# Setup of a two-block transformer kernel: small loads on a second queue, weights and modulation moved into the first turn

## The reference, cut to what matters

```python
# first block
tp = gelu(cond) @ Wt + bt
scale, shift = split(tp, 2)
h = layer_norm(x, ln1_g, ln1_b) * (1 + scale) + shift
q, k, v = split_heads(h @ Wqkv)
scores = q @ k.T / sqrt(16) - torus_dist * torus_scale[head]
x = x + merge(softmax(scores) @ v) @ Wout
x = x + gelu(layer_norm(x, ln2_g, ln2_b) @ W1 + b1) @ W2 + b2
# second block
ada = silu(cond @ ada1_w + ada1_b) @ ada2_w + ada2_b
shift1, scale1, gate1, shift2, scale2, gate2 = split(ada, 6)
a = attention(x, mask) @ proj_w + proj_b
x = x + gate1 * (layernorm(a) * (1 + scale1) + shift1)
m = gelu(x @ fc1_w + fc1_b) @ fc2_w + fc2_b
x = x + gate2 * (layernorm(m) * (1 + scale2) + shift2)
```

## Time and profile before

| | |
|---|---|
| runs before | 1455.85 us median of 3 (1454.34 to 1459.1) |
| the profiled execution | 1457.03 us, span of the trace 1455.2 us |
| granted TensorE clock, mean | 0.978 |
| first score matmul of turn 0 | 43.21 us |
| first score matmul of turn 1 | 127.69 us |
| TensorE busy over the span | 1309.6 us (90%) |
| HBM read and written | 72.64 MB, 58.75 MB |

### The profile page before, as it was taken

One profiled execution on the slowest core, in us unless ns is written; L12 is line 12 of the kernel. 1 busy time (PEld: TensorE's weight loads), 2 busy tenths in 40 slices (PEclk: granted clock), 3 DMA queues, 4 the chain that ended last, 5 costly groups with the idle time before them and its releaser, 6 DMA issues. The chain is left out here.

```text
span 1455.2 us, 24552 instructions
## 1 busy us (share of the span) xinstructions
PE 1309.6 (90%) x8789; PEld 1004.0 (69%) x8789; DVE 803.2 (55%) x2240; ACT 770.5 (53%) x1262; POOL 757.1 (52%) x939
## 2 busy tenths in 40 slices
PE   4898999999999999999999997989888898988777
PEld 3676777777777777777777775666666666665556
DVE  3766645645646656656645643464655556454452
ACT  3565665665665765665655752544544353453522
POOL 3788876776776776776776761020413222140323
PEclk9999999999999999999999998999999999999988
DMA  8432222223213213213213215353424242433100
GB/s 258 130 127 57 71 84 72 73 75 83 74 64 89 75 58 88 78 55 88 79 54 110 92 41 164 113 152 108 151 67 145 61 155 93 123 116 86 45 2 29
DMA packets 98259, 133.98 MB, mean 92 GB/s; under 512 B 16802, under 2 KB 51498, under 8 KB 98130
## 3 DMA queue, kind: packets, MB, share of 16 engines
q1 hardware_dynamic: 96850, 131.80, 30.3%
q10 hardware_dynamic: 1280, 0.53, 0.2%
HBM read 72.64 MB, written 58.75 MB: 90 GB/s over the span
## 5 line engine op out<-in xcount | busy, mean ns | idle before, releaser
L617 POOL TENSOR_SCALAR shifted<-shifted,row_max 128x512 f32<-128x512 f32 x512 | 360.6, 719 | 220.1 <-DVE row_max L1380 218.2
L1380 DVE CUSTOM_DVE_ANT_0 shifted<-score,bias 128x512 f32<-128x512 f32 x512 | 332.7, 687 | 255.4 <-PE score L855 165.6
L1091 ACT ACTIVATE probs<-turned 128x512 f32<-128x512 f32 x512 | 278.2, 596 | 211.4 <-PE turned L867 209.8
L867 PE MATMUL turned<-ident,shifted 128*128 128x128 f32 x2048 | 270.0, 275 | 6.8 <-POOL shifted L617 6.0
L867 PEld LDWEIGHTS turned<-ident,shifted 128*128 128x128 f32 x2048 | 233.6, 141 | 55.6 <-issue 26.6
L783 PE MATMUL dense<-w_down,hidden 128*128 128x256 f32 x1024 | 253.3, 383 | 0.8 <-ACT hidden L1072 0.8
L610 POOL TENSOR_SCALAR bias<-dist,scale 128x1024 f32<-128x1024 f32 x192 | 220.0, 1146 | 13.6 <-DMA down_bias<-in_L_cond_b 13.6
L855 PE MATMUL score<-k_rows,q_rows 97*128 97x512 f32 x512 | 205.2, 456 | 22.1 <-DVE row_max L1380 10.1
L783 PEld LDWEIGHTS dense<-w_down,hidden 128*128 128x128 f32 x1024 | 185.6, 191 | 32.6 <-issue 9.6
L763 PE MATMUL dense<-feat_m,w_up 128*128 128x512 f32 x768 | 188.4, 400 | 3.5 <-ACT hidden L1072 1.8
L763 PEld LDWEIGHTS dense<-feat_m,w_up 128*128 128x128 f32 x768 | 144.3, 192 | 37.1 <-ACT hidden L1072 5.3
(11 more groups left out here) (138 smaller groups left out, 1497.3 us busy)
## 6 DMA issues: line engine op xcount, KB each, us to landing
qk_rows<-qk_high SPq DMA_DIRECT2D x128, 256.0 KB
q_rows<-qk_rows SPq DMA_DIRECT2D x64, 384.0 KB
qk_rows<-qk_low SPq DMA_DIRECT2D x64, 256.0 KB
k_rows<-qk_rows SPq DMA_DIRECT2D x68, 192.0 KB
x_in_t<-in_x SPq DMA_DIRECT2D x8, 512.0 KB, 3.8
x_res<-in_x SPq DMA_DIRECT2D x8, 512.0 KB, 5.5
x_mid<-x_norm SPq DMA_DIRECT2D x8, 512.0 KB, 3.3
x_in_t<-x_mid SPq DMA_DIRECT2D x8, 512.0 KB, 3.9
```

The lines of the kernel that those rows point to most:

```text
L617: ins = pool.tensor_scalar(shifted[:, u % 3, i, :], shifted[:, u % 3, i, :], -1.0, row_max[:, t % 6:t % 6 + 1], ALU.mult, ALU.add)
L867: mm = pe.transpose(turned_bank[z % 2][:, HALF * kk + P * i:HALF * kk + P * i + P], shifted[:, u % 3, i, P * kt:P * kt + P], ident[:, :])
L1091: act.activation(probs[:, u % RING, 2 * pair:2 * pair + 2, :], turned_bank[z % 2][:, :].rearrange("p (a c) -> p a c", a=2), ACT.Exp)\
L1380: dve.tensor_tensor_reduce(shifted[:, u % 3, i, :], score_bank[t % 2], bias[:, u % 2, i, :], 1.0, 3.0e38, ALU.add, ALU.min, row_max[:, t % ...
```

## The change

1. The small loads of the prologue (cond in two parts, bt, ln1_g, ln1_b, ada1_b) are issued by ScalarE on its own queue. The one semaphore becomes three: `cond_loaded` (cond), `wt_loaded` (Wt) and `small_loaded` (bt, ln1).
2. SP's order changes. Behind x, the mask, Wt, Wqkv, torus_scale, ada1_w, the masks and torus_dist come at once x of batch 1, the stores and the row loads of groups 0 and 1. Then follow ada2_w, ada2_b, four transfers of constant rows, ln2, proj_b, b1 and b2.
3. VectorE applies batch 0's norm before the small operations for scale and shift.
4. The matmuls with ada2 leave the prologue: their three sets run in turn 0 behind the dense work of steps 3, 5 and 6 (`MODULATE`), all in the bank `pv_bank`, each behind the addition of the set before. VectorE adds at the step after (behind its own score tiles and dense work), makes the four products at step 9; `attend` at step 7 waits for the third addition, since it uses the same bank.
5. Wout, W1, the store of `mod_rows`, W2 and the store of the flag are issued by SP in turn 0 (`load_rest`), after x of batch 2 and before row group 2. Wout and W1 are staged in `hidden` (where ada2 was), ada2_b's sum lies in `w_down`. ScalarE splits both at step 17, VectorE at steps 18 and 19.
6. GpSimd waits for `down_loaded` at its first use of b2 and no longer in the prologue; the waits for ln2 and proj_b stand at step 0 of turn 1.

```diff
+    MODULATE = {3: 0, 5: 1, 6: 2}
+    SPLIT_AT = 17
...
-        ada = shifted[0:B, :, :, :].rearrange("p a b c -> p (a b c)")[:, 0:6 * D]
+        ada = w_down[0:B, :, :].rearrange("p a b -> p (a b)")[:, 0:6 * D]
...
             def prologue():
                 with nc.allow_non_contiguous_dma(reason="small vectors laid on partitions"):
                     load_x(0)
                     load_mask(0)
-                    load(cond_t[:, 0, :], d["cond_1024"][:, 0:P].rearrange("b p -> p b"), "cond_loaded")
-                    load(cond_t[:, 1, :], d["cond_1024"][:, P:D].rearrange("b p -> p b"), "cond_loaded")
-                    load(w_t, d["L0_cond_Wt"].rearrange("(c p) n -> p c n", p=P), "cond_loaded")
-                    load(bt_col[:, :], d["L0_cond_bt"].rearrange("(c p) -> p c", p=P), "cond_loaded")
-                    load(ln1_gb[:, 0, :], d["L0_cond_ln1_g"].rearrange("(c p) -> p c", p=P), "cond_loaded")
-                    load(ln1_gb[:, 1, :], d["L0_cond_ln1_b"].rearrange("(c p) -> p c", p=P), "cond_loaded")
+                    load(w_t, d["L0_cond_Wt"].rearrange("(c p) n -> p c n", p=P), "wt_loaded")
                     load(raw_qkv, d["L0_cond_Wqkv"].rearrange("(c p) n -> p c n", p=P), "wqkv_loaded")
                     load(scale[:, :], d["L0_cond_torus_scale"].unsqueeze(0).broadcast_to([P, H]), "dist_loaded")
+                    load(ada1, d["L1_cond_ada1_w"].rearrange("(c p) n -> p c n", p=P), "ada1_loaded")
+                    load(all_masks[:, :], d["mask_BxS_bk0"][:, 0:EARLY], "masks_loaded")
                     load(dist[:, :, :], d["L0_cond_torus_dist"][0].rearrange("(t p) k -> p t k", p=P), "dist_loaded")
-                    load(ada1, d["L1_cond_ada1_w"].rearrange("(c p) n -> p c n", p=P), "ada_loaded")
-                    load(ada1_col[:, :], d["L1_cond_ada1_b"].rearrange("(c p) -> p c", p=P), "ada_loaded")
+                    x_free(0)
+                    load_x(1)
+                    store_half(0, 0)
+                    store_half(0, 1)
+                    sp.wait_ge(s["ones_set"], 2)
+                    load_group(0, 0)
+                    store_half(0, 2)
+                    store_half(0, 3)
+                    load_group(0, 1)
+
                     load(ada2, d["L1_cond_ada2_w"].rearrange("(c p) n -> p c n", p=P), "ada_loaded")
                     load(ada, d["L1_cond_ada2_b"].unsqueeze(0).broadcast_to([B, 6 * D]), "ada_loaded")
...
+            def load_rest():
+
+                sp.wait_ge(s["ada_ready"], 3)
+                load(raw_out[0], d["L0_cond_Wout"].rearrange("(c p) n -> p c n", p=P), "wout_loaded")
+                load(raw_up[0], d["L0_cond_W1"].rearrange("(c p) n -> p c n", p=P), "wup_loaded")
                 sp.wait_ge(s["mod_ready"], 1)
                 sp.dma_start(mod_rows, mod_out).then_inc(s["mod_stored"], 16)
+                load_down("L0_cond_", "W2")
                 sp.wait_ge(s["flag_ready"], 1)
                 sp.dma_start(flags, early_flag[:, :]).then_inc(s["flag_stored"], 16)
-                for a in range(2):
-                    for x in range(2):
-                        at = PEAK_AT + 2 * a + x
-                        sp.dma_start(k_rows[at:at + 1, :, :, a, :].bitcast(F32),
-                                     q_rows[MASK_AT:KROWS, 0:2, :, :].bitcast(F32)).then_inc(s["row_ones"], 16)
...
                     x_free(n + 1)
                     load_x(n + 2)
+                if n == 0:
+                    load_rest()
                 load_group(n, 2)
...
             def attend(n, gq):
                 if gq == 0:
+                    if n == 0:
+                        pe.wait_ge(s["ada_step"], 3)
...
+            def modulation(c):
+
+                if c == 0:
+                    pe.wait_ge(s["ada_loaded"], 32)
+                    pe.wait_ge(s["silu_ready"], DC)
+                else:
+                    pe.wait_ge(s["ada_step"], c)
+                for k in range(DC):
+                    mm = pe.matmul(pv_bank[0:B, :], u_t[:, k, :], ada2[:, k, L * c:L * c + L],
+                                   start=(k == 0), stop=(k == DC - 1))
+                mm.then_inc(s["ada_ready"], 1)
...
                 pe.transpose(turned_bank[1][0:1, 0:B], early_max[:, :], ident[0:B, 0:B]).then_inc(s["early_turned"], 1)
-                pe.wait_ge(s["silu_ready"], DC)
-                for c in range(3):
-                    for k in range(DC):
-                        mm = pe.matmul((score_bank[0], score_bank[1], turned_bank[0])[c][0:B, :], u_t[:, k, :],
-                                       ada2[:, k, L * c:L * c + L], start=(k == 0), stop=(k == DC - 1))
-                    mm.then_inc(s["ada_ready"], 1)
-                pe.wait_ge(s["ada_step"], 3)
...
                     for piece, m in pieces(table, k, n):
                         dense(piece, m)
+                    if n == 0 and k in MODULATE:
+                        modulation(MODULATE[k])
...
+            def load(dst, src, loaded):
+                act.dma_start(dst, src).then_inc(s[loaded], 16)
+
             def prologue():
-                act.wait_ge(s["cond_loaded"], 16 * 6)
+                with nc.allow_non_contiguous_dma(reason="small vectors laid on partitions"):
+                    load(cond_t[:, 0, :], d["cond_1024"][:, 0:P].rearrange("b p -> p b"), "cond_loaded")
+                    load(cond_t[:, 1, :], d["cond_1024"][:, P:D].rearrange("b p -> p b"), "cond_loaded")
+                    load(bt_col[:, :], d["L0_cond_bt"].rearrange("(c p) -> p c", p=P), "small_loaded")
+                    load(ln1_gb[:, 0, :], d["L0_cond_ln1_g"].rearrange("(c p) -> p c", p=P), "small_loaded")
+                    load(ln1_gb[:, 1, :], d["L0_cond_ln1_b"].rearrange("(c p) -> p c", p=P), "small_loaded")
+                    load(ada1_col[:, :], d["L1_cond_ada1_b"].rearrange("(c p) -> p c", p=P), "ada1_loaded")
+                act.wait_ge(s["cond_loaded"], 16 * 2)
...
+                    if n == 0 and k == SPLIT_AT:
+                        take_high(w_out, raw_out[0], "wout_loaded", "out_high", 1)
+                        take_high(w_up, raw_up[0], "wup_loaded", "up_high", 1)
+                    if n == 1 and k == 0:
+                        act.wait_ge(s["rest_loaded"], 48)
...
                 first_norm("stats", 0, 0)
-                dve.wait_ge(s["cond_loaded"], 16 * 6)
+                first_norm("norm", 0, 0)
+                dve.wait_ge(s["small_loaded"], 16 * 3)
                 dve.wait_ge(s["tp_ready"], 1)
...
+            def add_modulation(c):
+                dve.wait_ge(s["ada_ready"], c + 1)
+                dve.tensor_tensor(ada[:, L * c:L * c + L], pv_bank[0:B, :], ada[:, L * c:L * c + L], ALU.add)\
+                    .then_inc(s["ada_step"], 1)
+
+            def modulation_rows():
...
+                    if n == 0 and k - 1 in MODULATE:
+                        add_modulation(MODULATE[k - 1])
+                    if n == 0 and k == 9:
+                        modulation_rows()
+                    if n == 0 and k == SPLIT_AT + 1:
+                        take_low(w_out, raw_out[0], "out_high", "out_split", 1)
+                    if n == 0 and k == SPLIT_AT + 2:
+                        take_low(w_up, raw_up[0], "up_high", "up_split", 1)
+                    if n == 1 and k == 0:
+                        dve.wait_ge(s["rest_loaded"], 48)
```

More of the change, by code:

```diff
@@ L211, in build @@
         raw_qkv_2 = [rows[:, :, :].rearrange("p a b -> p (a b)")[:, 0:3 * D] for rows in (x_norm, attn)]
-        raw_out = [staged[:, 6 * D:8 * D].rearrange("p (c n) -> p c n", c=DC),
+        raw_out = [hidden[:, 4, :].rearrange("p (c n) -> p c n", c=DC),
                    dist[:, 0, :].rearrange("p (c n) -> p c n", c=DC)]
-        raw_up = [staged[:, 8 * D:16 * D].rearrange("p (c n) -> p c n", c=DC),
+        raw_up = [hidden[:, 0:4, :].rearrange("p a b -> p (a b)").rearrange("p (c n) -> p c n", c=DC),
                   bias[:, :, :, :].rearrange("p c a b -> p c (a b)")]
@@ L424, in load, with load_biases, load_down @@
                 sp.dma_start(dst, src).then_inc(s[loaded], 16)
-            def load_down(pre, down, up_b, down_b):
-                load(w_down[:, :, :], d[pre + down].rearrange("(c p) n -> p c n", p=P), "down_loaded")
+            def load_biases(pre, up_b, down_b):
                 load(up_bias[:, :], d[pre + up_b].rearrange("(c p) -> p c", p=P), "down_loaded")
                 load(down_bias[:, :], d[pre + down_b].unsqueeze(0).broadcast_to([P, D]), "down_loaded")
+            def load_down(pre, down):
+                load(w_down[:, :, :], d[pre + down].rearrange("(c p) n -> p c n", p=P), "down_loaded")
             def prologue():
@@ L446, in prologue @@
+                    store_half(0, 1)
[4 more added lines that the diff above has]
+                    load_group(0, 1)
                     load(ada2, d["L1_cond_ada2_w"].rearrange("(c p) n -> p c n", p=P), "ada_loaded")
                     load(ada, d["L1_cond_ada2_b"].unsqueeze(0).broadcast_to([B, 6 * D]), "ada_loaded")
```

(24 more changed lines are left out.)

25 lines of the change are left out of this document (2 added, 23 removed).

## The result

The change made the kernel slower: 1482.75 us (median of 4 runs, 1480.19 to 1486.95) against 1455.59 us (median of 4, 1454.34 to 1459.1) for the kernel before, a ratio of 1.0182 with a 95% interval of 1.0153 to 1.0211. I had forecast 1463 and a range up to 1471: the sign is right, the size is not. The profiled execution has a span of 1480.3 us, 25.1 longer than before's.

What follows compares the result with a forecast made beforehand. TensorE bounds turn 0 (busy 79.2 of 84.5 us), a chain of loads and stores the prologue. -9.0 + 5.9 + 2.3 + 6.0 + 0.5 + 2.0 - 1.0 = +6.7 gave 1463 us, range 1450 to 1471.

Steps and rivals of the forecast that it cites:

- The start: Prologue: earlier loads let ScalarE read the first transposed piece at about 11.9 instead of 18.56, 6.7 us sooner.
- x_norm is made meanwhile: Prologue: the normalization moved ahead of the scale and shift operations is done by VectorE while TensorE's matmuls run.
- My rival of the second queue: Prologue: small loads on a second queue make nothing land sooner, only 3.4 us of issue gained; 1468 us, chance 0.11.
- The stores: Prologue: q and k stores no longer queue behind 3.8 MB of weights; with the earlier start, row loads issue 9.0 us sooner.
- until then the queue was full of weight loads: Prologue: explains why stores issued at 26.48 began to flow only near 30, 3.5 us later.
- R: Prologue: issue of the first row loads (q_rows<-qk_rows), 37.93 us in the kernel before, forecast at 28.9.
- The stop and the slow set: Turn 0, step 3: TensorE waits 5.9 us for ada2, then the first modulation set at low clock adds 2.3.
- Units 4 to 7: Turn 0: the attend at step 7 waits for VectorE's third addition behind unit 7, +6.0 us, bounds 3.6 and 8.8.
- Products: Turn 0, step 9: four small products, 1.4 us on VectorE, which is idle 36% of a plain stretch; +0.5 us.
- split: Turn 0, steps 17 to 19: splitting W1 and Wout blocks ScalarE, then VectorE; +2.0 us, bounds 0 and 4.
- catch-up: Rest of turn 0: TensorE makes up time later from its idle time in plain stretches, -1.0 us.
- The rest: Everything after turn 0: the other 1327.5 us taken as they are, no change in length.

Runs made afterwards that it cites:

- first experiment: Changed kernel with GpSimd's q_rows memset ahead of the statistics and k_rows' behind the coefficients: 1474.09 us, ratio to before 1.0116.
- all repairs: Changed kernel with memsets moved, bt and ln1 on SP behind Wqkv, ada2 and modulation in the prologue, W1 split in pieces: 1451.24 us, ratio 0.9956.
- the last two runs: Kernel before with norm ahead, memsets moved, small loads split over both queues: 1455.5 us; the same with W2, b1, b2 behind first row loads: 1451.1 us.
- the last run: Kernel before with norm ahead, memsets moved, small loads split over both queues, W2, b1, b2 behind the first row loads: 1451.1 us, ratio 0.9954.

## Why the prediction was wrong

*The start: failed.* The step is "x_norm is made meanwhile". I gave the moved norm its 1.37 us of the earlier trace rows and nothing else, and did not look at what GpSimd would be doing from 8.5 to 15.7. Moved there, it lasted 8.64 us and held back every VectorE operation behind it, tp first. Behind that block a second one lay hidden: the vectors on ScalarE's queue land 8.5 to 9.6 us after issue, where before they took 3.3 to 5.1, so tp could not start before 14.1 (first experiment). My rival of the second queue had the late vectors, but put the gain of the rest at 3.4; by the runs the start is worth nothing with the memsets in the way, 3.3 us with only the vectors late (43.21 to 39.91), and 5.1 with both repaired. The rule of the Trainium skill that I had weighed (DMA: Bandwidth & Descriptors, Issuing engines are not separate DMA queues) would have made 3.4. That is close to the 3.3, but by another mechanism: it counts issue time ahead of Wqkv, and the run waited for ln1_b's landing.

*The stores: failed.* The step is "until then the queue was full of weight loads". I read the 3.5 us between the first store's issue and the flow of 200 GB/s in that way, and took off 2.3 us when the loads are gone. From the first store's issue to R it is 11.45 us before, 11.17 in the changed kernel, 11.26 with the memsets moved, 11.33 with all repairs: at most 0.3 less, not 2.3. The transfers of the changed kernel from 26 to 38 us, in slices of 0.3 us and with no weights under way, show it:

```profile
GB/s 0 0 0 0 0 0 27 89 34 27 61 184 164 205 212 150 191 184 212 198 150 143 198 212 198 191 198 219 184 191 212 212 205 184 218 205 96 82 7 0
```

The first store is issued at 26.74 and its first bytes move near 27.8, but the rate of the earlier trace rows is reached only near 29.3, 2.6 us after the issue, though nothing stands ahead. The 1.2 us that I gave the stores to start came from no row. What sets the 2.6 us, and the 200 GB/s behind them, no run shows. In the kernel before, nothing held the first store back either:

```profile
21.38 3.71 SPq L424 DMA_DIRECT2D down_bias<-in_L_cond_b  x1
...
25.76 0.69 DVE L1341 SCALAR_TENSOR_TENSOR qk_low<-dense,qk_high 128x512 fp32r<-128x512 f32 x1 [3.71 <-ACT qk_high L1059]
```

SP is through with the bias loads at 25.09, VectorE ends qk_low at 26.45, and the store is issued at 26.48. What stands ahead of the stores costs something only when they are ready sooner: in the last two runs 2.7 us by SP's time to issue W2 and the bias loads, and 0.9 us on the way to R.

*The stop and the slow set: right, too small.* ada2 was issued at R+12.1, as forecast, and TensorE asked for it at R+13.6. It was there at R+21.8, not R+19.4. I had given it 360 GB/s to itself; it shared the DMA engines with the row group ahead of it and the bias loads behind (2.64 MB moved from 50 to 60 us, 1.57 of them ada2's), and the stretch moved 271 GB/s at a DMA share of 0.97. The half microsecond to complete came from no row. The next rows are the stop, the first set behind it, and the attend at step 7:

```profile
51.50:59.70 8.20, 0.04 (x1) 0.00 (x0) 1.31 (x4) 1.32 (x3) 3.91 (x6) 0.69 0.97 271
59.70:63.30 3.60, 3.59 (x5) 0.45 (x5) 0.00 (x0) 0.00 (x0) 0.00 (x0) 0.50 0.13 21
...
78.90:82.40 3.50, 3.44 (x33) 1.52 (x34) 0.01 (x1) 0.00 (x0) 1.07 (x1) 0.57 0.46 188
```

The set ran at a granted 0.50 (1.2 GHz) and took 3.58 us, as forecast (3.4).

*Units 4 to 7: right, too small.* 8.9 in place of 6.0, just above its upper bound of 8.8. The attend waited 2.59 us for the third addition, and the third set 1.28 for the second. Some 1.4 of it is the clock: behind the same wait the attend took 3.37 us at a granted 0.57 here, 3.23 at 0.60 with ada2 early and 2.42 at 0.77 with the small loads back on SP, but 1.93 or 1.94 at 1.00 in three other runs. One of these has the code of the changed kernel up to step 17 (the split in pieces), so this part differs from execution to execution.

*Products, split, catch-up: right, too small.* 1.9, 2.9 and -0.2, for 0.5, 2.0 and -1.0. VectorE's idle share, which I had offered as cover, lies where it waits for scores; what is put in its queue delays the row maxima, and TensorE waits for those at 89.85 and 119.29. Hardly anything was caught up: from unit 24 on the turn takes 24.0 us, 24.2 before.

*The rest:* nothing expected, 0.9 measured, within the spread of single executions. The bounds of the terms, as the prediction states them, add up to about -2.6 and +15.9, not -3.5 and +18; the measured +25.1 of the profiled executions lies outside both.

## What to carry to other kernels

Before an operation is moved earlier, read what the neighbouring engines do in the time it moves into, not only what its own engine does: a 1.4 us norm became 8.6 us beside two memsets. Work belongs in a wait that is there anyway (here for the rows' trip through DRAM), not in a turn in which TensorE is busy for 94% of the time; cover by an average idle share is no cover. And when a load seems to hold another back, look whether it is the bytes or the issuing queue's time: here 8 us of issuing, 7 of them for two small bias loads, delayed the first store by 2.7 us, while the 1.25 MB of Wout and W1 that stayed ahead of the stores in the last run cost about 0.5 (first score 38.66 against 38.13 with all repairs, where ada2 stands ahead as well).

## What the runs showed of the hardware

- VectorE's normalization (128x256, float32, memory to memory) and GpSimd's memset do not run together. An operation of 0.40 us lasts up to 3.68 us behind a memset of 3.51, and 1.12 behind one in pieces; the whole memset keeps its length. Beside GpSimd's bias tiles the same shows: 1.13 us for the last operation of the normalization, and 0.89 for one on tp at 17.32 that takes 0.17 in the first experiment. ScalarE's copy of Wqkv (1.48 us at 9.07) ran beside the same memset at its usual length (1.48 at 9.06 in the first experiment, with no memset beside it), and so did VectorE's subtraction for its low half beside k_rows' memset (1.75 us at 14.96 in the first experiment).
- Loads of one or two KB that are laid one element to a partition land late beside bulk transfers of another queue: bt and ln1 took 8.5 to 9.6 us on ScalarE's queue with torus_dist and Wqkv on SP's, 6.7 to 7.0 us on SP behind Wqkv, and 3.2 to 5.0 us on SP ahead of Wqkv (the small loads back on SP). Whether the queue or the bulk that was issued by then makes the difference, the runs do not separate.
- SP was held 3.09 and 4.13 us by the issue of b1 (4 KB) and b2 (128 KB written) behind the weights. In the changed kernel they took 0.43 and 2.20 us (55.03 and 55.50), in the last run 0.58 and 3.08; what sets these times no run shows.
- After the same idle of 2.59 us the attend took 1.93 or 1.94 us in three executions, at a granted 1.00, and 2.42, 3.23 and 3.37 in three, at 0.77, 0.60 and 0.57.
